# Looping over units with an eight-tile ring: an unrolled normalisation kernel rolled up, two units a turn

## What is computed

```python
def _gn(v, G=32, eps=1e-5):            # group norm: 2 channels a group, for each image
    g = v.reshape(B, G, C // G, H, W)
    m, s = mean(g, axis=(2, 3, 4)), var(g, axis=(2, 3, 4))
    return ((g - m) / sqrt(s + eps)).reshape(v.shape)

def _L0_conv_ref(x):                   # masked batch norm, x is _gn's output
    m = x.sum(axis=1) != 0             # places whose sum over all 64 channels is not zero
    n = m.sum(axis=(1, 2)); Nmax = n.max(); pad = Nmax - n
    total = B * Nmax
    # mean and var of each channel over the places in m, with x[:, :, 0, 0] once more for each of pad
    inv = 1.0 / sqrt(var + 0.001)
    out = where(m, x * inv, x)
    out[:, :, 0, 0] = where(pad > 0, x[:, :, 0, 0] * inv, out[:, :, 0, 0])
    return out

return x + _L0_conv_ref(_gn(x))
```

## Time and profile before

| | us |
|---|---|
| median of 3 runs | 1295.04 (1294.75 to 1295.29) |
| the profiled execution | 1294.88 |
| its span, first to last instruction | 1293.2 |

### The profile page before, as it was taken

One profiled execution on the slowest core, in us unless ns is written; L12 is line 12 of the kernel. 1 busy time (PEld: TensorE's weight loads), 2 busy tenths in 40 slices (PEclk: granted clock), 3 DMA queues, 4 the chain that ended last, 5 costly groups with the idle time before them and its releaser, 6 DMA issues.

```text
span 1293.2 us, 10692 instructions
## 1 busy us (share of the span) xinstructions
PE 741.7 (57%) x2882; PEld 302.4 (23%) x2882; DVE 796.5 (62%) x1892; ACT 816.4 (63%) x950; POOL 535.1 (41%) x504
## 2 busy tenths in 40 slices
PE   0766654566545665456654566544665446654475
PEld 0222222222222222122221222212222122222232
DVE  6776666566665666655666556665566655666563
ACT  0777555775557755567655676556765567755575
POOL 0055333454334544345443444434443444533450
PEclk9988767887678876688766887667887678866788
DMA  9999999999999999999999999999999999999997
GB/s 378 415 421 420 421 421 421 422 420 420 421 421 421 420 421 421 421 421 420 421 421 421 421 421 420 421 420 421 421 421 421 420 420 421 418 421 418 420 414 281
DMA packets 135469, 537.58 MB, mean 416 GB/s; under 512 B 4336, under 2 KB 4336, under 8 KB 135408
## 3 DMA queue, kind: packets, MB, share of 16 engines
q1 hardware_dynamic: 69936, 276.83, 52.3%
q10 hardware_dynamic: 65472, 260.05, 49.0%
HBM read 268.44 MB, written 268.44 MB: 415 GB/s over the span
## 4 chain that ended last, share of the span: by engine, by line
DMA 60%; ACT 15%; PE 11%; DVE 7%; issue 5%; SPq 0%; ACTq 0%
DMA out_dram<-slots 37%; DMA slots<-in_x_dram 23%; ACT slots L346 11%; PE flush L421 6%; ACT fresh L343 4%; DVE stats L471 2%; DVE spread L454 2%; PE stay L417 1%; PE stay L418 1%; PE small_ps L386 1%; PE small_ps L396 1%; DVE dev L517 1%; PE small_ps L397 1%; ACT sums L343 0%; SPq L237 0%
## 5 line engine op out<-in xcount | busy, mean ns | idle before, releaser
L471 DVE BATCH_NORM_STATS2 stats<-slots 128x6 f32<-128x512 f32 x1024 | 631.5, 680 | 437.8 <-DMA slots<-in_x_dram 436.5
L346 ACT ACTIVATE slots<-slots,out_bias,out_scale 128x1024 f32<-128x1024 f32 x512 | 622.4, 1245 | 2.3 <-DVE out_bias L528 1.3
L325 POOL TENSOR_TENSOR sums<-fresh,sums 128x512 f32<-128x512 f32 x360 | 458.8, 1274 | 363.6 <-ACT fresh L343 363.6
L421 PE MATMUL flush<-slots,weights 128*64 128x512 f32 x1536 | 442.0, 695 | 42.2 <-ACT fresh L343 40.6
L343 ACT ACTIVATE fresh<-flush,group_bias 128x512 f32<-128x512 f32 x360 | 246.5, 685 | 51.8 <-PE flush L421 51.8
L302 POOL TENSOR_TENSOR weights<-pair_sum,group_rstd 128x256 f32<-128x256 f32 (+1 forms) x128 | 73.2, 602 | 357.5 <-DVE group_bias L508 357.5
L421 PEld LDWEIGHTS flush<-slots,weights 128*64 128x64 f32 x1536 | 131.7, 156 | 295.9 <-issue 294.3
L358 ACT ACTIVATE by_image<-by_image,eps 128x16 f32<-128x16 f32 x32 | 9.8, 307 | 242.2 <-DVE by_image L495 241.8
L417 PE MATMUL stay<-slots,weights 128*64 128x512 f32 x512 | 140.0, 606 | 0.0
L418 PE MATMUL stay<-minus_mean,weights 128*64 128x512 f32 x512 | 138.1, 593 | 0.0
L386 PE MATMUL small_ps<-spread,group_avg 128*128 128x64 f32 x64 | 21.8, 443 | 183.3 <-DVE spread L491 183.3
(11 more groups left out here) (52 smaller groups left out, 234.5 us busy)
## 6 DMA issues: line engine op xcount, KB each, us to landing
slots<-in_x_dram SPq DMA_DIRECT2D x127, 2048.0 KB, 17.7
out_dram<-slots ACTq DMA_DIRECT2D x124, 2048.0 KB, 29.9
out_dram<-slots SPq DMA_DIRECT2D x16, 512.0 KB, 5.1
slots<-in_x_dram SPq DMA_DIRECT2D x4, 512.0 KB, 13.6
```

Of the source, the lines that this page charges most:

```text
L325: pool.tensor_tensor(into, fresh[:, n % FRESH_BUFS, :], into, ALU.add).then_inc(added, 1)
L346: nc.scalar.activation(out_in_ring(u, i), image_in_ring(u, i), ACT.Identity, bias=out_bias[:, u % 2, i:i + 1], scale=out_scale[:, u % 2, i ...
L421: nc.tensor.matmul(into, weight, source, start=True, stop=True).then_inc(image_summed, 1)
L471: last = V.bn_stats(stats[:, u % 2, k * BLOCK_STATS:(k + 1) * BLOCK_STATS], source)
```

## The change

Every engine's stream gets a loop. Unit 0 is written out, then a loop of 15 turns does units 1 to 30, two a turn (`LAP = 2`), then unit 31 is written out. SP's loads go likewise: eight written out, 14 turns of eight, eight at the end. A wait's value in the loop is the turn's number times the growth in one turn, plus a constant (`in_turn`), so it is computed in registers; the addresses in DRAM are as well. The addresses on chip must be the same in each turn, so the ring has eight tiles, exactly two units. The two places that this leaves hold the unit matrix and, at the end, four images of the last unit's result and the comparison with zero. As `group_mean` and `group_rstd` would be indexed by the turn on DVE, DVE now writes small tiles in two copies (`mean_now`, `rstd_now`), and POOL copies these to the tables, ahead of the weights. POOL's wait for `image_summed` is for the first image of the unit before, not for the last of two units before. `added` starts at `ADDED_TOKEN` = 12, so that every wait on it has a positive value. Where DVE counts its steps, the wait's value comes from a register too.

```diff
-RING = 10
+RING = 8
+PLACES = 10
+LAP = 2
...
+        def in_turn(value, it, by_unit):
+            assert value > 0
+            return value if it is None else it * (LAP * by_unit) + value
...
-            for j in range(TILES):
-                if j == RING - 1:
-
-                    sp.wait_ge(matrices_ready, MATRICES)
-                if j >= RING:
-                    sp.wait_ge(stored[j % RING], 16 * (j // RING))
-                if j < TILES - 1:
-                    sp.dma_start(in_ring(j), in_dram(x_rows, j)).then_inc(loaded[j % RING], 16)
+            def load(j, it=None):
                 if j >= RING:
+                    sp.wait_ge(stored[j % RING], 16 * (j // RING) if it is None else it * 16 + 16 * (j // RING))
+                sp.dma_start(in_ring(j), in_dram(x_rows, j, it)).then_inc(loaded[j % RING], 16)
+
+            for j in range(RING):
+                load(j)
+            with sp.Fori(0, (UNITS - 2 * LAP) // LAP) as it:
+                for j in range(RING, 2 * RING):
+                    load(j, it)
+            for j in range(TILES - RING, TILES - 1):
+                load(j)
...
-            for u in range(UNITS):
-                pool.wait_ge(rstd_ready, u + 1)
-                if u >= 2:
-                    wait_for_sum(pool, u - 2, B - 1)
+            def unit(u, it=None):
+                pool.wait_ge(rstd_ready, in_turn(u + 1, it, 1))
+                at = slice(u * B, (u + 1) * B) if it is None else bass.ds(it * (LAP * B) + u * B, B)
+                pool.tensor_copy(group_mean[:, at], mean_now[:, u % 2, :])
+                pool.tensor_copy(group_rstd[:, at], rstd_now[:, u % 2, :])
+                if u:
+                    wait_for_sum(pool, u - 1, 0, it)
...
-            def store(u, t):
+            def store(u, t, it):
                 j = u * UNIT_TILES + t
-                act.wait_ge(out_ready, (j + 1) * TILE_IMAGES)
-                act.dma_start(in_dram(out_rows, j), in_ring(j)).then_inc(stored[j % RING], 16)
+                act.wait_ge(out_ready, in_turn((j + 1) * TILE_IMAGES, it, B))
+                act.dma_start(in_dram(out_rows, j, it), in_ring(j)).then_inc(stored[j % RING], 16)
...
+            unit(0)
+            with act.Fori(0, (UNITS - LAP) // LAP) as it:
+                for u in range(1, 1 + LAP):
+                    unit(u, it)
+            unit(LAST)
...
-                return steps[0]
+                return steps[0] if turn[0] is None else turn[0] * lap_steps[0] + steps[0]
```

More of the change, by code:

```diff
@@ L53, in norm_conv_kernel @@
     SMALLS = 4
+    ADDED_TOKEN = ADDS
+    assert ADDS % FRESH_BUFS == 0 and ADDS % FLUSH_BANKS == 0
     WEIGHT_PARTS = B // EVERY
@@ L318, in _ @@
                 if 0 < u < LAST:
[L319 to L325, removed]
+                    for k, i in enumerate(flushed):
+                        pool.wait_ge(taken, in_turn(taken_with(u, i), it, ADDS))
+                        pool.wait_ge(added, in_turn(ADDED_TOKEN + taken_with(u - 2, i), it, ADDS))
+                        into = sums[:, k, :]
+                        pool.tensor_tensor(into, fresh[:, k % FRESH_BUFS, :], into, ALU.add).then_inc(added, 1)
+            pool.sem_inc(added, ADDED_TOKEN)
+            unit(0)
+            with pool.Fori(0, (UNITS - LAP) // LAP) as it:
+                for u in range(1, 1 + LAP):
+                    unit(u, it)
+            unit(LAST)
             pool.nop()
@@ L421, in channel_sums, with unit @@
                             nc.tensor.matmul(into, weight, source, start=True, stop=True).then_inc(image_summed, 1)
-            for u in range(UNITS):
-                statistics(u)
-                channel_sums(u)
+            def unit(u, it=None):
+                statistics(u, it)
+                channel_sums(u, it)
+            unit(0)
+            with pe.Fori(0, (UNITS - LAP) // LAP) as it:
+                for u in range(1, 1 + LAP):
+                    unit(u, it)
+            unit(LAST)
             small(UNITS * SMALLS + 1, count_ps, group_avg[:, :], n_row)
@@ L438, in _ @@
             V = nc.vector
-            steps = [0]
+            steps, turn, lap_steps = [0], [None], [0]
             def note(ins):
@@ L530, in _, with unit @@
             AHEAD = 6
-            for u in range(UNITS):
+            def unit(u, it=None):
                 for k in range(AHEAD if u else 0, UNIT_BLOCKS):
-                    block_stats(u, k)
+                    block_stats(u, k, it)
                 ahead = [0]
                 def meanwhile(n):
-                    if u + 1 < UNITS:
+                    if u < LAST:
                         for k in range(ahead[0], ahead[0] + n):
-                            block_stats(u + 1, k)
+                            block_stats(u + 1, k, it)
                     ahead[0] += n
-                statistics(u, meanwhile)
+                statistics(u, meanwhile, it)
                 assert ahead[0] == AHEAD
+            unit(0)
+            TURNS = (UNITS - LAP) // LAP
+            lap_steps[0] = LAP * steps[0]
+            with dve.Fori(0, TURNS) as turn[0]:
+                for u in range(1, 1 + LAP):
+                    unit(u, turn[0])
+            turn[0] = None
+            steps[0] += (TURNS - 1) * lap_steps[0]
+            unit(LAST)
             def count(i):
```

131 lines of the change are left out of this document (67 added, 64 removed).

## The result

| | before | after |
|---|---|---|
| median | 1295.03 us (4 runs) | 1345.11 us (4 runs, 1337.80 to 1357.61) |
| profiled execution | 1294.88 | 1357.61 |
| its span | 1293.2 | 1355.9 |

The ratio is 1.0397, with a 95% interval from 1.0309 to 1.0484: 4% slower, where 1344 us was forecast. The runs of the change spread over 20 us, those of before over half a microsecond. The profiled execution is the slowest of the four, 12.5 us above the median, so what its trace shows of a unit is a little longer than in the median run.

The account below looks back on a forecast made before the run. Transfers bound the kernel before; with eight tiles the ring's way round would: 10.0 + 13.9 + 16.6 + 1.0 = 41.5 us a unit. Span 46.0 + 30 x 41.5 + 50.8 = 1341.8, forecast 1344 us, range 1308 to 1388.

Parts of the forecast that it names:

- the four legs: Ring's way round per unit: store, load's issue after landing, load, chain to next first store; 41.5 us with register work.
- store: A unit's first store, from issue to landing, partly sharing the DMA engines with loads: 10.0 us.
- load: Load of tile 4u+8 behind that store, sharing the DMA engines with stores throughout: 13.9 us.
- the chain with its register work: DVE, PE and ACT from the landed tile to the unit's first store: 16.6 us plus register work.
- The loops' 1.0 us: Register work for waits on the way round: 0.54 us on ACT and SP, 0.48 on DVE, together 1.0 a unit.
- the sign given for it (17.0 to 17.6 us): Expected trace evidence of register work: 17.0 to 17.6 us from DVE's first block to the first store.
- The 0.3 us allowed for a transfer whose address is in a register: In the upper end of register work, about 4 us: some 0.3 us each for a load and a store.
- Branches: Loop branches, once in two units, dearest 0.237 us: hidden in the engines' waits, costed at nothing.
- POOL, start and end: POOL's two copies 0.8 us, costing nothing; first store at 46.0 us; unit 30's first store to span's end 50.8 us.
- The bytes stay the limit: Rival: legs shorter than read, period 39.9 us, 1296 to 1308 us, 1300 say; chance 0.13.
- Control costs more: Rival: register work, register addresses or fetches at turns make the period 43 to 45 us, 1405 us say; chance 0.13.
- Faster: Rival: loops drop nearly all instruction fetches, 2.6 us of the DMA engines' span, giving 1292.3 us; chance 0.03.

Follow-up runs that it names:

- e12: The change again, unaltered: 1345.79 us, ratio 1.0386 to the kernel before.
- e1: The kernel before, unrolled, with a ring of eight tiles and the change's two places beside the ring, no loops: 1356.99 us, ratio 1.0505.
- e4: The change with DVE taking no block of the next unit amid its statistics, so the unit's own last tile starts them: 1298.39 us, ratio 1.0028.
- e7: The change with the chain 2.04 us longer, by three more reads of the next unit's first block: 1366.07 us, ratio 1.0547.
- e8: The kernel before with the chain 2.04 us longer, by three more reads of the next unit's first block: 1295.20 us, ratio 1.0002.
- e5: The change with POOL's two copies behind its weight products instead of ahead of them: 1352.52 us, ratio 1.0451 to the kernel before.
- e6b: The unrolled kernel with a ring of eight (e1), with two copies on POOL put ahead of the weight products: 1351.62 us, ratio 1.0438 to the kernel before.
- e2: The change with a ring of ten tiles and ten units a turn, loops and register work kept: 1303.68 us, ratio 1.0067 to the kernel before.
- e3: The kernel before, unrolled, with a ring of nine tiles and e1's edit: 1299.45 us, ratio 1.0030.
- e9: The kernel before, ring of ten, with DVE taking no block of the next unit amid its statistics: 1294.76 us, ratio 0.9998.

## Why the prediction was right

**The total.** 1344 against 1345.11 (and 1345.79 in e12). The mechanism is shown: the four legs follow each other without a pause; e1 brings the loss without loops, e4 takes it away with ring and loops in place, e7 and e8 show that a longer chain counts with eight tiles and not with ten. That the total is right to 1 us is luck. The ten runs lie between 1335.1 and 1357.6, and the terms are off in both directions: in the profiled execution by +1.3 (store), +0.4 (load) and -1.1 us a unit (the chain with its register work, 16.35 for 17.4).

**The legs.** Load 14.31 for 13.9, close. Store 11.26 for 10.0, the term that was undersized. I had worked one unit by itself, with the last load of the unit before nearly done. Really short and long periods mostly take turns. After the short one of 38.9 us the unit's last load lands 11.7 us after the next first store is issued, and that store takes 14.4 us; after a long one of 43.9 us it lands 4.0 us after, and the store takes 9.0. The mean lies above what one unit shows.

**The loops' 1.0 us.** Wrong, and it made up for the store leg. Register work was priced at fused work's 0.213 us, one instruction that works on a value just loaded from memory. In the loop (ns):

```profile
L251 SPq FUSED_REGOPS  x112: 37/37/72, 52.3 to 1217.2; - x112
...
L491 DVEq ALU_OP  x375: 40/40/40, 68.2 to 1298.0; - x188
```

0.037 and 0.040 us. Of DVE's, those between linked operations vanish beside the operation; only the one at L543, which carries a wait itself, is seen, as 0.09 us more. On SP it is 0.17 with the move behind it, 0.15 more than before. And the chain got shorter by 0.3 us, not longer by 0.8, so the sign given for it (17.0 to 17.6 us) failed; e5 and e6b put most of that down to POOL's products starting after DVE's. The 0.3 us allowed for a transfer whose address is in a register rested on no row; an issue takes 0.383 us where it took 0.379, with a MOVE of 0.029 ahead of it. "A gain is excluded, since no wait of the chain is dropped" was the false sentence: durations can change without any wait.

**Branches.** 0.05 us on ACT, 0.06 on DVE, 0.21 on PE, and no fetch from turn to turn: from 300 to 1250 us the instruction queues are silent. Costed at nothing, and so it is. The Trainium skill's rule (Runtime: NRT & Kernel Launch, Instruction fetch mechanics) is that a jump out of the two pages held forces a fetch. The traces agree, with e2's 5.5 us and its instruction packets at the jump over a body five times as long; how long a body may be no run here shows.

**POOL, start and end.** The copies put the weights off by 0.3 us (747.39 to 747.70) where 0.8 was taken, and PE doesn't wait for it, as said. First store at 45.6 for 46.0; last 50.2 us for 50.8, since the last stores land in 5.0 us (6.3 at most) where it was 12.8 at most.

**The rivals.** "The bytes stay the limit" falls with 398 GB/s; it nearly holds for nine tiles (e3, 417). "Control costs more" falls with the rows above. "Faster" falls: the fetches did go, but nothing came of it, in e4 neither, where the way round is out of play and the time is 0.3% above the kernel before.

## What to carry to other kernels

In a ring of buffers, write down the way round once: from a store's issue over its landing, the load into its place, and all that must happen until the next store of that kind. While that sum is under the time that the bytes need, it costs nothing to lengthen it; one buffer less may push it over, and then everything on it counts. Look for what waits for the *freshest* buffer: here taking six blocks of work early, harmless with ten tiles (e9), was what made eight too few, and without it a loop with eight tiles is within 0.3% of the unrolled kernel. As to loops, the jump was nearly free for a body of two units (on DVE 167 records of the trace), and cost each of four engines 4.9 to 5.9 us for one of ten units.

## What the runs showed of the hardware beyond that

The DVE product `spread<-stats,by_image` over 128 x 64 that starts while POOL works on a product of 128 x 256 ends 0.08 us after POOL's. Before, this is so in 31 of 32 units: in the earlier trace rows POOL's first product starts at 661.36, DVE's just after it, and DVE's takes 0.65 us; started before POOL's it takes 0.24 (747.32 above). It is not only operations of two inputs: the TENSOR_SCALAR `dev<-dev,small_ps` takes 0.46 us beside POOL's products before, and 0.24 to 0.26 in 25 of 32 units of the change (0.59 to 0.72 in the rest). Block statistics kept their 0.69 us beside the same work.

The time of the change spreads over 22 us (1335.1 to 1357.6 in ten runs), none of them between 1341.1 and 1350.2; that of the kernel before spreads over one. Eight tiles alone don't do it: e4 has them too and spreads over 4 us, e7 over 4, e5 and e6b over 8 and 7. Why the change spreads so was not tried.
